# First stage of a four-layer transformer kernel: one product per norm, the gains applied by VectorE, the squares summed by ScalarE

## What is computed

```python
q = (x @ Wq).reshape(B, L, H, d)
feat = jax.nn.elu(q) + 1.0
KV = jnp.einsum('nshd,nshv->nhdv', feat, q / L)
Z = 1.0 / (jnp.einsum('nlhd,nhd->nlh', feat, feat.sum(axis=1)) + ATTN_EPS)
msg = jnp.einsum('nlhd,nhdv,nlh->nlhv', feat, KV, Z) * L
msg = msg.reshape(B, L, D) @ Wm
x = x + _layernorm(msg, g1, b1)
mlp = jax.nn.relu(msg @ W1) @ W2
x = x + _layernorm(mlp, g2, b2)
...
x = _layernorm(x_in + x)        # then the router's logits, the eight best experts and their weights
```

## Time and profile before

| | us |
|---|---|
| median of three runs | 703.17 |
| lowest, highest | 703.03, 703.64 |
| the profiled execution's own time | 702.37 |
| its span | 700.6 |
| TensorE busy in the span | 587.2 (84%) |
| VectorE busy | 437.3 (62%) |
| ScalarE busy | 274.0 (39%) |
| GpSimd busy | 442.0 (63%) |
| mean granted TensorE clock | 0.852 of full |

### The profile page before, as it was taken

The page is one execution under the profiler, slowest core; times in us unless marked ns, Lnnn a source line. Parts: engine busy times, 40 slices in busy tenths (PEclk is TensorE's granted clock), DMA queues, the critical chain, the costliest instruction groups (busy, mean ns, idle before and its releaser), DMA issues.

```text
span 700.6 us, 10473 instructions
## 1 busy us (share of the span) xinstructions
PE 587.2 (84%) x3201; PEld 473.7 (68%) x3201; DVE 437.3 (62%) x1480; ACT 274.0 (39%) x559; POOL 442.0 (63%) x479
## 2 busy tenths in 40 slices
PE   5998999379299986365999989988989899999882
PEld 4797888335188775255777777867877787788662
DVE  2465778689634435534576767667667666775762
ACT  3465565215122223331634435345435353363331
POOL 6353444617677775644777867967868859652573
PEclk9999899659755555587999989999989989999996
DMA  4697475579022124330300300300203000000000
GB/s 121 175 300 292 190 270 220 195 170 206 10 72 65 60 67 146 124 120 1 121 1 9 127 1 8 128 9 13 115 8 127 1 8 8 1 16 0 10 7 16
DMA packets 47221, 61.98 MB, mean 88 GB/s; under 512 B 13026, under 2 KB 39873, under 8 KB 46146
## 3 DMA queue, kind: packets, MB, share of 16 engines
q1 hardware_dynamic: 44610, 56.15, 25.3%
q0 software_dynamic: 2560, 5.23, 2.6%
HBM read 35.16 MB, written 24.13 MB: 85 GB/s over the span
## 4 chain that ended last, share of the span: by engine, by line
PE 57%; DVE 18%; issue 8%; ACT 8%; DMA 4%; POOL 3%; SPq 1%; DVEq 0%; POOLq 0%; ACTq 0%
PE pair L1218 8%; PE pair L1220 7%; PE pair L1219 7%; PE pair L1450 5%; DVE c_g L1071 3%; DVE cand L1649 3%; PE pair L1460 2%; DVE keyT L1651 2%; PE pair L1324 2%; PE pair L467 2%; PE pair L1313 2%; PE pair L1717 2%; PE pair L1318 2%; ACT c_sg L940 2%; PE pair L511 2%
## 5 line engine op out<-in xcount | busy, mean ns | idle before, releaser
L854 POOL TENSOR_TENSOR c_acc<-c_acc,c_g 128x512 f32<-128x512 f32 x112 | 144.0, 1286 | 65.9 <-DVE c_g L1071 60.4
L940 ACT ACTIVATE c_sg<-pair 128x512 f32<-128x512 f32 x128 | 76.4, 597 | 161.6 <-PE pair L1220 161.3
L1071 DVE SCALAR_TENSOR_TENSOR c_g<-pair,c_comb,c_sg 128x256 f32<-128x256 f32 x224 | 97.6, 478 | 63.9 <-ACT c_sg L940 62.7
L1218 PE MATMUL pair<-c_w_hi,c_x3h 128*128 128x512 f32 x256 | 117.0, 457 | 9.3 <-DVE c_g L1071 6.6
L1220 PE MATMUL pair<-c_w_hi,c_x3l 128*128 128x512 f32 x256 | 105.8, 413 | 0.0
L1219 PE MATMUL pair<-c_w_lo,c_x3h 128*128 128x512 f32 x256 | 105.6, 412 | 0.0
L1218 PEld LDWEIGHTS pair<-c_w_hi,c_x3h 128*128 128x128 f32 x256 | 52.0, 203 | 25.6 <-DVE c_g L1071 13.4
L1220 PEld LDWEIGHTS pair<-c_w_hi,c_x3l 128*128 128x128 f32 x256 | 51.1, 200 | 12.7
L1219 PEld LDWEIGHTS pair<-c_w_lo,c_x3h 128*128 128x128 f32 x256 | 52.1, 204 | 8.0
L1534 POOL DMA_INDIRECT rows_all<-token_rows,tok_row x32 | 31.2, 976 | 12.6 <-issue 8.2
L1539 POOL DMA_INDIRECT routed_rows<-x1T_all,dest_row x32 | 32.3, 1008 | 9.8 <-issue 8.5
(11 more groups left out here) (326 smaller groups left out, 1499.0 us busy)
## 6 DMA issues: line engine op xcount, KB each, us to landing
routed_rows<-rows_all SPq DMA_DIRECT2D x8, 2048.0 KB
c_c<-routed_rows SPq DMA_DIRECT2D x7, 2048.0 KB, 7.7
token_rows<-a_xw SPq DMA_DIRECT2D x8, 384.0 KB, 3.1
a_x<-in_L_attn_x SPq DMA_DIRECT2D x8, 256.0 KB, 3.3
base_all<-a_xw SPq DMA_DIRECT2D x8, 256.0 KB, 3.5
c_c<-routed_rows SPq DMA_DIRECT2D x4, 512.0 KB, 5.1
out<-c_outb SPq DMA_DIRECT2D x16, 128.0 KB, 1.8
wgu_late<-in_L_ffn_w_gate SPq DMA_DIRECT2D x4, 480.0 KB, 7.1
```

The lines of the kernel that those rows point to most:

```text
L854: g.tensor_tensor(acc, acc, b["g"][:, (2 * uf + i) % 4, :, :], ALU.add).then_inc(s["acc"], 1)
L940: a_.activation(b[f"sg{q % 2}"][:, :, :], self.pair[q % 2][:, :, H1:2 * H1], SIG).then_inc(s["sig"], 1)
L1071: ins = v.scalar_tensor_tensor(out=dst, in0=self.pair[q % 2][:, x, 0:H1], scalar=b[f"comb{uf}"][:, j * E1 + e:j * E1 + e + 1], in1=b[f"sg{ ...
L1218: t.matmul(dst, w_hi, x_hi, start=start, stop=False)
```

## The change

One product per norm is left: `Wmc` into bank 3 and `W2c` into bank 4, both without gains. ScalarE takes the squares straight from these banks in four instructions of 128 x 128 per norm instead of one of 128 x 512, and each gives its sum into one column of `var` through the accumulator output. VectorE's two sums are gone; in their places `gain` multiplies bank 3 by g1 (into `gm`) and bank 4 by g2 (into `gl`) in SBUF. The adds read `gm` and `gl` instead of PSUM. The weights with gains and their two set-up products are gone.

```diff
+        def square_sums(name, src, at):
+            for j in range(NT):
+                c = slice(j * D, (j + 1) * D)
+                ins = a.activation(b[name][:, c], src[:, c], ACT.Square, scale=float(1.0 / np.sqrt(D)), accum_out=b["var"][:, at + j:at + j + 1])
+            return ins
...
                 act.wait_ge(s["m2_mm"], n + 1)
                 if n:
-                    act.wait_ge(s["var_m"], n)
-                a.activation(b["sqm"][:, :], bank[2][:, :], ACT.Square, scale=float(1.0 / np.sqrt(D))).then_inc(s["sqm_sb"], 1)
+                    act.wait_ge(s["var_eps"], n)
+                square_sums("sqm", bank[3], 0).then_inc(s["var_m"], 1)
...
                 act.wait_ge(s["l_mm"], n + 1)
-                if n:
-                    act.wait_ge(s["var_l"], n)
-                a.activation(b["sql"][:, :], bank[5][:, :], ACT.Square, scale=float(1.0 / np.sqrt(D))).then_inc(s["sql_sb"], 1)
+                square_sums("sql", bank[4], NT).then_inc(s["var_l"], 1)
...
-            v.tensor_tensor(b["Wmg"][:, :], b["Wmc"][:, :], b["g1"][:, :], ALU.mult)
-            v.tensor_tensor(b["W2g"][:, :, :], b["W2c"][:, :, :], bcast_mid(b["g2"][:, :], 2), ALU.mult).then_inc(s["setup_dve"], 1)
+        def gain(name, n):
+            src, g = (bank[3], b["g1"]) if name == "m" else (bank[4], b["g2"])
+            dve.wait_ge(s["var_" + name], n + 1)
+            if n:
+                dve.wait_ge(s["add"], 2 * n)
+            v.tensor_tensor(b["g" + name][:, :].rearrange("p (j d) -> p j d", d=D), src[:, :].rearrange("p (j d) -> p j d", d=D),
+                            bcast_mid(g[:, :], NT), ALU.mult).then_inc(s[f"g{name}_sb"], 1)
...
-                dve.wait_ge(s["sqm_sb"], n + 1)
-                if n:
-                    dve.wait_ge(s["var_eps"], n)
-                v.tensor_reduce(b["var"][:, 0:NT], b["sqm"][:, :].rearrange("p (j d) -> p j d", d=D), AX.X, ALU.add).then_inc(s["var_m"], 1)
+                gain("m", n)
...
-                dve.wait_ge(s["sql_sb"], n + 1)
-                v.tensor_reduce(b["var"][:, NT:2 * NT], b["sql"][:, :].rearrange("p (j d) -> p j d", d=D), AX.X, ALU.add).then_inc(s["var_l"], 1)
+                gain("l", n)
...
-                        ins = v.scalar_tensor_tensor(out=r[:, c], in0=bank[bk][:, c], scalar=b["rstd"][:, at + j:at + j + 1], in1=r[:, c], op0=ALU.mult, op1=ALU.add)
+                        ins = v.scalar_tensor_tensor(out=r[:, c], in0=b["g" + name][:, c], scalar=b["rstd"][:, at + j:at + j + 1], in1=r[:, c], op0=ALU.mult, op1=ALU.add)
...
                 if n:
-                    pe.wait_ge(s["add"], 2 * n - 1)
+                    pe.wait_ge(s["gm_sb"], n)
                 for j in range(NT):
-                    ins = t.matmul(bank[3][:, j * D:(j + 1) * D], b["msgT"][:, j * P:(j + 1) * P], b["Wmg"][:, :], start=True, stop=True)
-                if k < self.N:
-                    pe.wait_ge(s["feat_sb"], k + 1)
-                    pe.wait_ge(s["q_sb"], k + 1)
-                for j in range(NT):
-                    ins = t.matmul(bank[2][:, j * D:(j + 1) * D], b["msgT"][:, j * P:(j + 1) * P], b["Wmc"][:, :], start=True, stop=True)
+                    ins = t.matmul(bank[3][:, j * D:(j + 1) * D], b["msgT"][:, j * P:(j + 1) * P], b["Wmc"][:, :], start=True, stop=True)
                 ins.then_inc(s["m2_mm"], 1)
...
+                if n:
+                    pe.wait_ge(s["gl_sb"], n)
                 for j in range(NT):
                     for h in range(2):
-                        ins = t.matmul(bank[5][:, j * D:(j + 1) * D], b["hT"][:, h, j * P:(j + 1) * P], b["W2c"][:, h, :], start=(h == 0), stop=(h == 1))
+                        ins = t.matmul(bank[4][:, j * D:(j + 1) * D], b["hT"][:, h, j * P:(j + 1) * P], b["W2c"][:, h, :], start=(h == 0), stop=(h == 1))
                 ins.then_inc(s["l_mm"], 1)
-                if n:
-                    pe.wait_ge(s["add"], 2 * n)
-                for j in range(NT):
-                    for h in range(2):
-                        ins = t.matmul(bank[4][:, j * D:(j + 1) * D], b["hT"][:, h, j * P:(j + 1) * P], b["W2g"][:, h, :], start=(h == 0), stop=(h == 1))
-                ins.then_inc(s["lg_mlp_mm"], 1)
```

More of the change, by code:

```diff
@@ L101, in __init__ @@
         k("g1", [P, D]); k("g2", [P, D]); k("b12", [P, 2, D])
-        k("WmT", [P, D]); k("WmW1", [P, 2 * D]); k("Wmc", [P, D]); k("Wmg", [P, D]); k("W2c", [P, 2, D]); k("W2g", [P, 2, D])
+        k("WmT", [P, D]); k("WmW1", [P, 2 * D]); k("Wmc", [P, D]); k("W2c", [P, 2, D])
         k("wmu", [P, 4]); k("headmask", [P, D + H0])
@@ L109, in __init__ @@
         k("kvs", [P, D + H0]); k("z", [P, 2, 2, H0]); k("msg", [P, NT * D]); k("msgT", [P, L]); k("hT", [P, 2, L])
-        k("sqm", [P, NT * D]); k("sql", [P, NT * D]); k("var", [P, 2 * NT]); k("rstd", [P, 2 * NT])
+        k("sqm", [P, NT * D]); k("sql", [P, NT * D]); k("gm", [P, NT * D]); k("gl", [P, NT * D]); k("var", [P, 2 * NT]); k("rstd", [P, 2 * NT])
         k("st3", [P, 6 * NT]); k("mv3", [P, 2 * NT]); k("rstd3", [P, NT]); k("nmu", [P, NT])
@@ L114, in __init__ @@
             xT_mm xT_sb q_mm negq eq q_sb feat_sb featT_mm featT_sb kv_mm kvs_sb num_mm z_step msg_sb msgT_mm msgT_sb
-            hT_mm m2_mm hT_sb sqm_sb var_m l_mm lg_mlp_mm sql_sb var_l var_eps rstd r_half r_step add st3 mv3 rstd3_step
+            hT_mm m2_mm hT_sb var_m gm_sb l_mm var_l gl_sb var_eps rstd r_half r_step add st3 mv3 rstd3_step
             x1_sb x1T_mm x1T_kept lgt_mm lg_sb pick d_sb ex_sb mask_sb w_sb maskT_mm maskT_sb rank_mm key_sb""".split()}
@@ L274, in act @@
                 if n:
-                    act.wait_ge(s["lg_mlp_mm"], n)
+                    act.wait_ge(s["l_mm"], n)
                 a.activation(b["hT"][:, 0, :], bank[5][:, :], ACT.Relu).then_inc(s["hT_sb"], 1)
@@ L350, in setup @@
             ins.then_inc(s["setup_dve"], 1)
-            dve.wait_ge(s["setup_dve"], 3)
-            v.tensor_tensor(b["Wmg"][:, :], b["Wmc"][:, :], b["g1"][:, :], ALU.mult)
-            v.tensor_tensor(b["W2g"][:, :, :], b["W2c"][:, :, :], bcast_mid(b["g2"][:, :], 2), ALU.mult).then_inc(s["setup_dve"], 1)
+        def gain(name, n):
[5 more added lines that the diff above has]
+                            bcast_mid(g[:, :], NT), ALU.mult).then_inc(s[f"g{name}_sb"], 1)
         for k in range(self.N + 3):
@@ L453, in dve @@
                 dve.wait_ge(s["r_step"], n + 1)
-                for name, bk, at in (("m", 3, 0), ("l", 4, NT)):
+                for name, at in (("m", 0), ("l", NT)):
+                    dve.wait_ge(s[f"g{name}_sb"], n + 1)
                     if name == "l":
@@ L492, in pe @@
                 pe.wait_ge(s["xT_sb"], n + 1)
-                if n >= 2:
-                    pe.wait_ge(s["sqm_sb"], n - 1)
                 if n >= 5 and n % 2:
@@ L506, in pe @@
                     pe.wait_ge(s["setup_act"], 3)
-                    pe.wait_ge(s["setup_dve"], 4)
+                    pe.wait_ge(s["setup_dve"], 3)
                 if n >= 2:
@@ L568, in pe @@
                 pe.wait_ge(s["maskT_sb"], m // 2 + 1)
-                if k - 1 < self.N:
-                    pe.wait_ge(s["sqm_sb"], k)
                 if m == 1:
@@ L577, in pe @@
                 pe.wait_ge(s["x1T_kept"], n + 1)
-                if k - 1 < self.N:
-                    pe.wait_ge(s["sql_sb"], k)
-                else:
+                if k - 1 >= self.N:
                     pe.wait_ge(s["lg_sb"], n)
```

## The result

The changed kernel took 696.05 us in the median of 20 runs (694.22 to 701.63); the kernel before, run beside it, 701.91 in 20 runs (696.28 to 706.37). The ratio is 0.9934 with a 95% interval of 0.9911 to 0.9958: 4.6 us faster, 3.0 to 6.2. The forecast was 705.1, slower by 2. It was wrong in sign, and 696.05 lies outside its range.

What follows compares the result with a forecast made beforehand. With the products gone, VectorE's path, only 0.50 us behind TensorE's, was taken to bound the turns. Shifts of -1.0 and clock +3.0 gave +2.0 on 702.37, 704.4; on the runs' median 703.17, 705.1 us, range 700 to 709.

Steps and rivals of the forecast that it cites:

- TensorE can give back at most 0.50 us of the 2.71 in a turn like the third: First stage, turn 3: VectorE's path has only 0.50 us of slack to TensorE's, so removing 2.71 us saves at most that.
- Step of a square 0.29, from 0.18 to 0.39: ScalarE's four squares per norm start 0.29 us apart, the middle taken; VectorE may start its step 0.68 us later.
- L360 waits 2.0 us, message transposes 1.5 us: VectorE's product waits 2.0 us for the MLP's squares instead of 1.32; TensorE's message transposes wait 1.5 for VectorE.
- Adds from SBUF cost the same and lie behind the message, with slack: VectorE's eight adds, reading SBUF in place of PSUM, were taken at the same 2.28 us, without a row of that form.
- Odd turns of 13.1 us, turn 6 not shorter: First stage, q to q: turns 3, 5 and 7 +0.2 us each, 13.1; turn 6 -0.6, at 13.14.
- Turn 4: the store of image 0 comes 1.0 sooner: In turn 4 x1 waits for this store, which moves 1.0 us sooner; q(5) stands at -0.3 in all.
- The clock: 1.5 more low stretches at 2.0 us: TensorE idles where products went; one or two low-clock spells, likely after turns 5 and 7, add 3.0 us.
- the second rival: First stage: the clock holds and squares step by 0.29 us: -1.0 us, 702.2 us; chance 0.15.
- Sum of the first stage: +2.0: First-stage shifts of -1.0 us without the clock plus 3.0 for the clock, on the profiled 702.37: 704.4 us.
- The first (cheap accumulators, 699.1): Hand-over from MLP squares to VectorE: square step 0.18, path grows only 0.24 us, clock holds: -4.1, 699.1 us; chance 0.15.
- The fourth (TensorE still last): TensorE still ends last in the first stage's turns, so removing its products gives -21.7 us; chance 0.02.
- the last 0.06: Low-clock spells in more turns and shifted ones in later stages: above 709 us; chance 0.06.

Runs made afterwards that it cites:

- cut_back: The changed kernel ended after its first stage, with TensorE's second products put back as work that nobody reads: 159.96 us.
- cut_after: The changed kernel ended after its first stage, the rest left out: 159.22 us.
- cut_early: The changed kernel ended after its first stage, with VectorE's gain product over the MLP's output moved behind the message: 156.37 us.
- cut_acc: The kernel before, ended after its first stage, both products kept, squares summed by ScalarE's accumulators, VectorE's two sums gone: 157.24 us.

## Why the prediction was wrong

**The step that failed** is the choice of what to look at: "because the change touches the first 146 us only". From there the sum added up shifts of the first stage, and took what follows at its old cost. The change also shifted VectorE's program by 13 instructions, and that freed the last stage's loop from a stall of 2.5 us; with what hangs on it, this is the whole measured gain (0.9941 for the shift alone, 0.9934 for the change). The sign was lost there. With the stall put back, the change itself is worth 1.0008 (0.9981 to 1.0034), 702 to 706 us on 703.17, which the forecast range held. That it held is partly luck: two terms of the first stage were mis-sized and worked against each other (the adds and the store, below).

The trace of before had shown the stall, in the earlier trace rows: TensorE waiting 2.29 us at 474.34 for VectorE's `c_acc`. I used that row for the clock alone. It did not occur to me to ask why VectorE was late, and one row further the answer was "issue".

**Point by point in the first stage:**

- *TensorE can give back at most 0.50 us of the 2.71 in a turn like the third.* Borne out in the main: putting all 21.7 us back cost 0.7 us, the clock's recovery included (cut_back against cut_after, ranges overlapping). Turn 1 is another matter. It shrank from 12.42 to 10.56 us, 1.86 of the 2.71, and turn 2 took it back, with 2.15 us of TensorE waiting for x1 (14.81 in place of 12.96). q(3) came 0.2 sooner, forecast 0.5.
- *Step of a square 0.29, from 0.18 to 0.39.* It was 0.25: a 128-wide square and a separate read of the accumulator of 0.19 to 0.23 us that overlaps it. Four take 1.00, not 1.16.
- *L360 waits 2.0 us, message transposes 1.5 us.* 1.88 and 1.42: right. That this hand-over bounds the turn was right too: cut_early and cut_acc take it away and gain 2.8 and 1.6 us.
- *Adds from SBUF cost the same and lie behind the message, with slack.* Wrong, a term put at nothing without a row. All 64 adds before, and of those after the first four of each eight (shortest, median and longest in ns):

```profile
L459 DVE SCALAR_TENSOR_TENSOR a_r<-pair,a_rstd,a_r x64: 340/343/352, 30.3 to 128.5; 128x128 f32<-128x128 f32 x64
```

```profile
L464 DVE SCALAR_TENSOR_TENSOR a_r<-a_gm,a_rstd,a_r x32: 339/342/1427, 28.5 to 125.3; 128x128 f32<-128x128 f32 x32
```

The longest took 1.43 us in place of 0.35. The long ones, one or two of the first two in each turn, are those that run beside GpSimd's two steps on `r`:

```profile
42.82 3.00 DVE L464 SCALAR_TENSOR_TENSOR a_r<-a_gm,a_rstd,a_r 128x128 f32<-128x128 f32 x4
...
42.76 1.03 POOL L230 TENSOR_TENSOR a_r<-a_x 128x512 f32<-128x512 f32 x1
43.86 1.27 POOL L232 TENSOR_TENSOR a_r<-a_r,a_b 128x512 f32<-128x512 f32 x1
```

Eight adds take 4.2, 4.2, 3.4, 3.0, 3.4, 3.0 and 3.4 us in turns 1 to 7, and 2.4 in turn 8, where GpSimd is idle; in the kernel before they took 2.3 beside the same GpSimd steps. All 64 are busy 30.1 us in place of 22.0. In turn 3 the slack was 0.28 us: in the kernel before, `feat` (L361) at 46.57 us stood behind the adds and waited that long for ScalarE's exp. In cut_after, whose clock is full until the turn's last 0.3 us, `feat` starts 3.69 us behind q in place of 2.72, TensorE's transposes of it wait 0.71 us for VectorE, and the turn takes 14.2 us. No run has the gains with adds that read PSUM, so how the 2.7 us between cut_acc and cut_back divide between the adds and the kept wait is not shown.
- *Odd turns of 13.1 us, turn 6 not shorter.* Turn 3 took 13.92, turn 5 13.44 and turn 6 13.33 (before: 12.96, 14.00, 13.74).
- *Turn 4: the store of image 0 comes 1.0 sooner.* Mis-sized. ScalarE's x1 waited until 65.12, not 67.62, 2.5 sooner, and q(5) to q(7) came 2.8, 3.3 and 3.7 us sooner than before in that profile:

```profile
65.12 1.26 ACT L309 ACTIVATE a_xw<-a_r,a_nmu,a_rstd 128x128 f32<-128x128 f32 x3 [1.39 <-DMA base_all<-a_xw]
```

SyncE did not begin to issue that store sooner; it issued it faster, 0.71 us in place of 2.59. Before and after:

```profile
60.38 2.59 SPq L196 DMA_DIRECT2D base_all<-a_xw  x1
```

```profile
60.41 0.71 SPq L196 DMA_DIRECT2D base_all<-a_xw  x1
```

The write of zeros ahead of it went out 1.6 us sooner (55.33 in place of 56.89), which may have emptied the queue; no run shows the cause.

- *The clock: 1.5 more low stretches at 2.0 us.* The mechanism was right. In turns 2 and 4 and behind turn 7's waits the granted clock fell to half, where before it did so once up to 124 us: 13.6 us at the low level in place of 6.8. The forecast had it behind turns 5 and 7. The windows of the kernel after:

```profile
42.20:45.60 3.40, 2.98 (x15) 2.84 (x15) 3.31 (x6) 0.96 (x2) 2.86 (x3) 0.51 1.05 292
69.70:72.90 3.20, 3.20 (x17) 3.15 (x16) 3.17 (x8) 0.83 (x2) 2.41 (x3) 0.50 0.02 5
110.60:117.20 6.60, 4.91 (x10) 2.45 (x11) 6.43 (x29) 1.18 (x2) 2.84 (x6) 0.50 0.98 370
```

The last costs 1.8 us on the path, since the products of `WmW1` and the message took 3.78 us there in place of 1.98:

```profile
113.40 3.78 PE L514 MATMUL pair<-a_msgT,a_WmW 128*128 128x512 f32 x4 [0.68 <-ACT a_msgT L339]
```

The rule of the Trainium skill that VectorE's copies do not break the array's warmth (TensorE: Matmul & The Clock Gate, Loop structure matters more than you think), which the second rival followed, did not keep the clock up here: over the stage it went from 0.97 to 0.91. In the Trainium skill's sketch the next products follow at once; in this stage they wait for VectorE and ScalarE.

- *Sum of the first stage: +2.0.* Measured +0.4 between the cut kernels, their ranges overlapping. (On 703.17 the sum gives 705.2, not 705.1.) The store and the square's step gained more than forecast; the adds, put at nothing, and the clock took it back. How much each took is not separated.

**The rivals.** The first (cheap accumulators, 699.1) is nearest in time, for a reason that did not occur: its squares step by 0.18 us and save 4.1 in the first stage, measured are 0.25 and no gain. The fourth (TensorE still last) is excluded by cut_back. None of them looked beyond the first stage, except the last 0.06, and that on the slow side.

How the 0.6% divides: the fourth step of the last stage (from the start of one image's gated output to the next) holds the jump. It took 48.7, 49.6, 51.2 and 48.8 us in the four profiles with the stall, and 46.1, 45.8, 47.1, 47.1, 46.4 and 46.4 in the six without, all on chips where before takes 700 to 703 us: 49.6 against 46.5 in the mean, 3.1 us. The shift of the loop alone is worth 4.1 us (0.9941 on 702.47); the remaining 1.0 is not located, and low-clock stretches behind it move a profile by more than that.

## What to carry to other kernels

Compare two profiles over their whole length, stage by stage, before any cause is named: an edit can move time in code that it does not touch, by the number of instructions ahead of a loop. When a kernel has a hardware loop, look at "issue" gaps behind each jump and at instruction loads beside them; a dozen idle instructions, or the loop written out, may be worth more than the edit itself. When a wait is read, ask once more why the engine waited for was late. And when a change moves an operand to another memory, the same instruction is a new one: find a row of it, with the neighbours that it will have, before it is put at no cost.

## What the runs showed of the hardware

- **A jump back can cost 2.9 us or 0.3 us by the place of the loop in the program.** With a pass of 358 instructions on VectorE, a start at 800, 823 or 876 stalled (2.85 to 2.93 us from the branch to the next register instruction) and one at 836 or 964 did not (0.32 to 0.35). The Trainium skill says, in Runtime: NRT & Kernel Launch, section Instruction fetch mechanics, that a taken branch whose target is outside the pages held forces a fetch before execution goes on. The three instruction loads beside the stall agree. The size that it gives for a page, 16 KiB, does not fit the queue that loads beside VectorE's stall: the page of the profile after has 25 loads of 0.20 MB in all on the queue that took part, 8 KB each, and 20 of 0.33 MB, 16 KB each, on the other:

```profile
q8 instruction: 20, 0.33, 0.2%
q14 instruction: 25, 0.20, 0.1%
```

- **An accumulator output of ScalarE is an instruction of its own**, ACTIVATION_READ_ACCUMULATOR, 0.19 to 0.23 us on [128,1]; it overlaps its square and the next one, and 128-wide squares follow each other at 0.25 us.
- **An add with both inputs in SBUF was held up beside GpSimd's work, the same add from PSUM was not.** `scalar_tensor_tensor` of 128x128 took 0.97 to 1.43 us beside GpSimd's instructions of 1.03 and 1.27 us on `r`, and 0.34 to 0.35 with GpSimd idle (trace of the kernel after); reading PSUM it took 0.34 to 0.35 in both cases (trace of before).
- **TensorE's spare time can be paid for in clock, by where the waits fall.** With 21.7 us of products less, the granted clock over the first stage fell from 0.97 to 0.91; with idle products in their place it was 0.99, and the three cut kernels lie within 1.2 us. In cut_early, with as few products as cut_after (606 and 601 instructions) but TensorE's waits otherwise placed, it was 0.98:

```profile
5.00:124.00 119.00, 90.69 (x606) 75.15 (x605) 84.35 (x299) 72.65 (x245) 52.72 (x99) 0.98 0.70 228
```

- **Two chips differed by 2.6% with the same kernel** (before: 702.47 and 721.00 us); ratios taken on one chip were the only thing that could be compared.
